# Conv-attention layer and displaced blur: key/value units in two halves of each pair, x statistics moved into the projection, one tile of layer 1 per pair

## The reference

```python
# layer 0: x = x + attention(group_norm(x))
qkv = x_flat @ W_qkv.T            # 12 heads of 64; q is not used
var_v = jnp.var(v, axis=-1, ddof=1, keepdims=True)
var_k = jnp.var(k, axis=-1, ddof=1, keepdims=True)
scores = var_v @ jnp.swapaxes(var_k, -2, -1) * scale      # rank one: 1024 x 1024 per head
out = jax.nn.softmax(scores, axis=-1) @ v
out = out @ W_proj.T + b_proj
# layer 1: x = x + displace(group_norm(x)): each channel is shifted by whole pixels
# (zeros outside), then a 3 x 3 Gaussian with a sub-pixel centre is applied to it
```

## Time and profile before

| what | value |
|---|---|
| median of 3 runs | 2242.65 us (2242.59 to 2244.2) |
| profiled execution, its own time | 2248.03 us |
| its span, first to last instruction | 2246.5 us |
| mean granted TensorE clock | 0.959 |
| PE busy | 2061.6 us, 92% |
| PEld busy | 1101.4 us, 49% |
| DVE busy | 1680.9 us, 75% |
| ACT busy | 1179.2 us, 52% |
| POOL busy | 145.9 us, 6% |
| DMA, mean | 98 GB/s, 219.14 MB |

### The profile page before, as it was taken

The page is one execution under the profiler, slowest core; times in us unless marked ns, Lnnn a source line. Parts: engine busy times, 40 slices in busy tenths (PEclk is TensorE's granted clock), DMA queues, the critical chain, the costliest instruction groups (busy, mean ns, idle before and its releaser), DMA issues.

```text
span 2246.5 us, 36318 instructions
## 1 busy us (share of the span) xinstructions
PE 2061.6 (92%) x13036; PEld 1101.4 (49%) x13036; DVE 1680.9 (75%) x3695; ACT 1179.2 (52%) x1285; POOL 145.9 (6%) x215
## 2 busy tenths in 40 slices
PE   3999999998989999999999999999998999999970
PEld 2655356552655436553465525654365543755330
DVE  7577656886679875898659885788667987598738
ACT  5456625665266662567336662566526665356701
POOL 2000000000000000000001000000000000010001
PEclk7899999999999999999999999999999999999995
DMA  6312302433033511334023340244213341143304
GB/s 236 139 48 58 95 11 95 133 130 99 17 108 122 170 42 39 123 121 154 21 67 123 114 143 11 95 133 142 87 27 106 121 164 39 40 132 123 95 10 168
DMA packets 106990, 219.14 MB, mean 98 GB/s; under 512 B 53025, under 2 KB 53793, under 8 KB 106785
## 3 DMA queue, kind: packets, MB, share of 16 engines
q1 hardware_dynamic: 74816, 100.12, 14.9%
q0 software_dynamic: 25920, 94.38, 12.1%
q10 hardware_dynamic: 6048, 22.02, 2.6%
HBM read 158.28 MB, written 57.80 MB: 96 GB/s over the span
## 4 chain that ended last, share of the span: by engine, by line
PE 76%; DMA 7%; DVE 7%; ACT 3%; issue 3%; SPq 3%; ACTq 0%; DVEq 0%; POOL 0%; POOLq 0%
PE ps L1105 30%; PE ps L1144 25%; PE ps L1159 15%; PE ps L1126 5%; ACT ring L599 2%; DMA dt_sb<-d_sb 2%; DMA a_sb<-a_rows 2%; SPq L461 1%; DMA a_rows<-at 1%; DVE xv L859 1%; DVE xv L861 1%; DVE st L754 1%; SPq L400 1%; DVE bt L805 1%; DMA xv<-in_L_conv_W_qkv 1%
## 5 line engine op out<-in xcount | busy, mean ns | idle before, releaser
L599 ACT ACTIVATE ring<-a_sb,coef 128x1024 f32<-128x1024 f32 x768 | 834.3, 1139 | 404.7 <-PE ps L1144 215.7
L1105 PE MATMUL ps<-wkv_hi,h_sp 128*128 128x256 f16 x4608 | 806.2, 278 | 46.9 <-ACT xv L583 39.5
L1144 PE MATMUL ps<-ring,xv 128*64 128x512 f32 x3072 | 739.6, 612 | 0.7
L1105 PE MATMUL ps<-wkv_lo,h_sp 128*128 128x256 f16 x2304 | 639.7, 278 | 0.0
L1105 PEld LDWEIGHTS ps<-wkv_hi,h_sp 128*128 128x128 f16 x4608 | 458.4, 99 | 214.3 <-issue 122.5
L805 DVE TENSOR_TENSOR bt<-bt,ring 128x1024 f32<-128x1024 f32 x416 | 487.7, 1214 | 1.8 <-issue 1.8
L1144 PEld LDWEIGHTS ps<-ring,xv 128*64 128x64 f32 x3072 | 196.7, 138 | 381.2 <-issue 359.7
L1159 PE MATMUL ps<-xv,wp_hi 128*128 128x512 f16 x1152 | 347.4, 379 | 10.0 <-issue 9.6
L754 DVE BATCH_NORM_STATS2 st<-ps 128x6 f32<-128x64 f32 x1536 | 219.8, 217 | 116.5 <-PE ps L1105 115.6
L583 ACT ACTIVATE xv<-ps 128x256 f32<-128x256 f32 x192 | 70.9, 369 | 351.8 <-DVE st L754 351.6
L1105 PEld LDWEIGHTS ps<-wkv_lo,h_sp 128*128 128x128 f16 x2304 | 229.2, 99 | 28.9
(11 more groups left out here) (122 smaller groups left out, 1329.6 us busy)
## 6 DMA issues: line engine op xcount, KB each, us to landing
a_sb<-a_rows SPq DMA_DIRECT2D x96, 512.0 KB, 5.9
xv<-in_x POOLq DMA_DIRECT2D x48, 512.0 KB, 3.7
bt<-r_rows SPq DMA_DIRECT2D x96, 256.0 KB, 3.9
h_sp<-in_x ACTq DMA_DIRECT2D x42, 512.0 KB, 6.5
shift_rows<-bt POOLq DMA_DIRECT2D x42, 512.0 KB, 2.9
out<-xv POOLq DMA_DIRECT2D x42, 512.0 KB, 3.6
shift_rows<-ring SPq DMA_DIRECT2D x12, 528.0 KB, 14.8
xv<-in_L_conv_W_qkv SPq DMA_DIRECT2D x4, 1152.0 KB, 9.2
```

The source lines that it names most:

```text
L599: nc.scalar.activation(ring_of(p, s, m), a_sb[:, h % 4, :], ACT.Exp, scale=coef[:, h, m:m + 1]).then_inc(s_exp, 1)
L1105: last = nc.tensor.matmul(ps[:, kv_bank[u % 2], half * 2 * P:(half + 1) * 2 * P], h_sp[:, k, hp, m * P:(m + 1) * P], wkv[wpart][:, k, q * ...
L1144: last = nc.tensor.matmul(ps[s * HD:(s + 1) * HD, o_bank[p % 2] + j, :], v_sb[:, p, m, s * HD:(s + 1) * HD], ring_of(p, s, m)[:, j * HALF: ...
```

## The change

In pairs 0 to 3, PE makes two units, multiplies m = 0 to 3, makes two units, multiplies m = 4 to 7 (before: one unit after each of m = 0, 2, 4, 6). The transposes come before m = 0 (before: after m = 1), the spread after m = 2 (before: after m = 3). Unit 6 is evicted in phase A. ACT evicts units in twos at steps 3 and 7, DVE takes their statistics at steps 2, 3, 5 and 6 and makes the variances two pairs ahead at step 6. `k_max` moves from step 2 to step 3, behind an add and a unit's statistics. Tile p of layer 1 is done in pair p, at steps 3 and 6. `add_bias` moves to step 7, for tile 4 to the span's end. The six loads of the next x are issued in twos at steps 1, 4 and 7 of pair 4. The statistics of x move from pair 5 to the start of the projection, around the last reciprocal, and the DMAs of their chain on SP behind the last broadcast of r. `o_second` of a pair comes at step 7 of the next. The projection first takes k = 0 to 3 of units 2 to 5, then k = 4 of all six.

```diff
--- before.py
+++ after.py
@@ -429,14 +429,12 @@
                     r_broadcast(b, p - 1, later)
                     if p < NP - 1:
                         a_broadcast(b, p + 1, later)
+                d_rows(b, NP - 1)
+                r_write(b, NP - 1)
+                r_broadcast(b, NP - 1, later)
                 if with_next:
                     stats_to_groups(sp, "x", b + 1)
-                d_rows(b, NP - 1)
-                r_write(b, NP - 1)
-                if with_next:
                     stats_out(sp, "x", b + 1)
-                r_broadcast(b, NP - 1, later)
-                if with_next:
                     stats_to_channels(sp, "x", b + 1)

             def first():
@@ -571,8 +569,8 @@
                     if t:
                         h_first(b, t - 1)

-            def load_x(b):
-                for t in range(CT):
+            def load_x(b, tiles):
+                for t in tiles:
                     act.dma_start(x_in[:, t, :], x_t[b, :, t, :]).then_inc(s_xin[t], 16)

             def v_evict(b, u):
@@ -623,7 +621,7 @@
                 nc.scalar.activation(t_t, g_t, ACT.Copy, scale=taps[:, t, 1, 1:2]).then_inc(s_tap, 1)

             def phase_a(b, beside=None):
-                for u in range(2 * UQ - 2):
+                for u in range(2 * UQ - 1):
                     v_evict(b, u)
                     if beside is not None:
                         beside(u)
@@ -631,42 +629,39 @@
             def span(b, l1, with_next, beside=None):
                 later = l1 is not None
                 for p in range(NP):
-                    nxt = (p + 1) * UQ
+                    nxt = (p + 2) * UQ
                     for m in range(MT):
                         if not later and p == 0 and m == 3:
                             act.wait_ge(s_pads, 2 * CT * 16)
                         exps(b, p, m)
-                        if m == 0 and 1 <= p <= 4:
-                            v_evict(b, nxt + 1)
-                        if m == 1 and p == 0 and later:
-                            middle_tap(l1, 0)
-                        if m == 2 and p <= 4:
-                            v_evict(b, nxt + 2)
+                        if m == 1 and p == 0:
+                            v_evict(b, 2 * UQ - 1)
                         if m == 3:
                             if p:
                                 d_copy(b, p - 1, later)
-                            if p <= 4:
-                                v_evict(b, nxt + 3)
-                            if p == 4 and with_next:
-                                load_x(b + 1)
-                        if m == 4 and 1 <= p <= 4 and later:
-                            middle_tap(l1, p + 1)
-                        if m == 5 and p:
-                            add_bias(b, p - 1)
-                        if m == 6 and p <= 3:
-                            v_evict(b, nxt + UQ)
+                            if later:
+                                middle_tap(l1, p)
+                            if p <= 3:
+                                v_evict(b, nxt)
+                                v_evict(b, nxt + 1)
                         if m == 7:
                             if p:
                                 o_first(b, p - 1)
-                            elif later:
-                                middle_tap(l1, 1)
+                            if 1 <= p <= 4:
+                                add_bias(b, p - 1)
+                            if p <= 3:
+                                v_evict(b, nxt + 2)
+                                v_evict(b, nxt + 3)
+                        if with_next and (p, m) in ((4, 1), (4, 4), (4, 7)):
+                            load_x(b + 1, (2 * (m // 3), 2 * (m // 3) + 1))
                         if beside is not None:
                             beside(p, m)

             def span_end(b, later):
                 d_copy(b, NP - 1, later)
+                add_bias(b, CT - 2)
+                o_first(b, NP - 1)
                 add_bias(b, CT - 1)
-                o_first(b, NP - 1)

             def weight_first(u):
                 parts, sc, t, k, r, bank = w_unit(u)
@@ -684,7 +679,7 @@
             def beside_span(p, m):

                 if (p, m) == (0, 0):
-                    for w in range(2 * (2 * UQ - 2 - 2), WU - WKU):
+                    for w in range(2 * (2 * UQ - 1 - 2), WU - WKU):
                         weight_first(WKU + w)
                 if (p, m) == (1, 0):
                     act.wait_ge(s_sub, 1)
@@ -887,65 +882,55 @@
             def span(b, l1, with_next, beside=None):
                 later = l1 is not None
                 for p in range(NP):
-                    nxt = (p + 1) * UQ
-                    if p >= 2:
-                        o_second(b, p - 2)
-                    if p <= 4:
-                        kv_stats(b, nxt + 3)
-                        variances(b, p + 1)
+                    nxt = (p + 2) * UQ
+                    if p == 0:
+                        kv_stats(b, 2 * UQ - 1)
+                        variances(b, 1)
                     for m in range(MT):
                         add_up(b, p, m, later)
-                        if m == 1 and p == 5 and with_next:
-                            x_stats(b + 1, (0, 1))
                         if m == 2:
                             if p:
                                 d_reciprocal(b, p - 1)
+                            if p <= 3:
+                                kv_stats(b, nxt)
+                        if m == 3:
+                            if p <= 3:
+                                kv_stats(b, nxt + 1)
                             if p <= 4:
                                 k_max(b, p + 1, later)
-                            if p == 0 and later:
-                                taps_y(l1, 0, g_t, t_t)
-                                gn(l1, 1, g_t)
-                                taps_x(l1, 0, t_t)
-                            if p == 5 and with_next:
-                                x_stats(b + 1, (2, 3))
-                        if m == 3:
-                            if p <= 3:
-                                kv_stats(b, nxt + UQ)
-                            if p == 5 and with_next:
-                                x_stats(b + 1, (4, 5))
-                                channel_aggregate("x", b + 1)
+                            if later:
+                                taps_y(l1, p, g_t, t_t)
+                                if p + 1 < CT:
+                                    gn(l1, p + 1, g_t)
                         if m == 4:
+                            if p <= 4:
+                                k_scales(b, p + 1)
                             if p:
                                 o_normalise(b, p - 1)
-                            if p <= 4:
-                                k_scales(b, p + 1)
-                        if m == 5:
-                            if p <= 3:
-                                kv_stats(b, nxt + UQ + 1)
-                            if 1 <= p <= 4 and later:
-                                taps_y(l1, p + 1, g_t, t_t)
-                                if p + 2 < CT:
-                                    gn(l1, p + 2, g_t)
+                        if m == 5 and p <= 3:
+                            kv_stats(b, nxt + 2)
                         if m == 6:
                             if p <= 3:
-                                kv_stats(b, nxt + UQ + 2)
-                            if p == 0 and later:
-                                taps_y(l1, 1, g_t, t_t)
-                                gn(l1, 2, g_t)
-                            if p <= 4 and later:
-                                taps_x(l1, p + 1, t_t)
+                                kv_stats(b, nxt + 3)
+                                variances(b, p + 2)
+                            if later:
+                                taps_x(l1, p, t_t)
+                        if m == 7 and p:
+                            o_second(b, p - 1)
                         if beside is not None:
                             beside(p, m)

             def group_end(b, with_next):
-                o_second(b, NP - 2)
+                if with_next:
+                    x_stats(b + 1, range(4))
+                d_reciprocal(b, NP - 1)
+                if with_next:
+                    x_stats(b + 1, (4, 5))
+                    channel_aggregate("x", b + 1)
+                o_normalise(b, NP - 1)
+                o_second(b, NP - 1)
                 if with_next:
                     group_var(dve, "x", b + 1)
-                d_reciprocal(b, NP - 1)
-                if with_next:
-                    group_spread_x(dve, b + 1, H_UP)
-                o_normalise(b, NP - 1)
-                o_second(b, NP - 1)
                 for u in range(PU):
                     t, j = divmod(u, 2)
                     dve.wait_ge(s_pj, b * PU + u + 1)
@@ -954,8 +939,10 @@
                     cut = x1[:, t, j * HALF:(j + 1) * HALF]
```

(29 more changed lines are left out.)

## The result

| | before | after |
|---|---|---|
| median | 2242.62 us (4 runs, 2239.26 to 2244.2) | 2203.53 us (4 runs, 2201.6 to 2208.88) |
| profiled execution, its span | 2248.03, 2246.5 us | 2203.28, 2201.7 us |
| mean granted TensorE clock | 0.959 | 0.965 |
| PE, DVE, ACT busy | 92%, 75%, 52% | 92%, 76%, 53% |

The ratio of the new time to the old is 0.9831 [0.9811, 0.9852]: faster, as predicted, and inside the range. The sum was made for the profiled execution, 2203.5 us, and that took 2203.28; the forecast for the median, 2198, is 5 us low. In the second set of runs, on the chip of the first experiments, the same kernel gave 0.9854. The experiments are set against the ratio of the same set of runs where there is one, else against 0.984, the middle of the two; 0.001 is 2.2 us. The two ratios of the changed kernel lie 0.0023 apart, so a difference against 0.984 is known to some 3 to 5 us only.

The account below looks back on a forecast made before the run. PE, 92% busy, waited for V and `kdiag`; after the change the DVE-ACT-rows loop sets pairs 1 to 4. Six middle batches -39.3, last +1.7, batch 0 -6.9: -44.5, so 2203.5 us profiled, 2198 median; range 2170 to 2236.

Parts of the forecast that it names:

- The loop: Pairs 1 to 4: DVE from the reciprocal, ACT exponentials, `d_copy`, row DMAs, next reciprocal; 33.6 us against PE's 32.5; chance 0.58.
- After `kdiag`: Pair 4: from `kdiag` to the pair's end 15.8 us, before 14.1, with one product more behind it.
- The merging pays nothing there: Pairs 1 to 4: PE's merged runs make a pair 32.5 instead of 33.4 us, but the loop sets the pace.
- The early eviction: Pair 0: `v_evict` 6 moved ahead of the exponentials, so unit 8 needs nothing more; pair 0 takes 32.5 instead of 40.4.
- The load term: Pair 4: two loads of the next x meet the denominators' rows and lengthen their trip by 1.2 us, bounds 0 and 3.8.
- Projection and phase A: Start of a batch: 73.6 us plus 0.5, as the late subtraction readies tile 5 1.9 after the projection's end.
- The last batch: Batch 7, which has no load: 258.4 us, before 256.7, so +1.7.
- Batch 0: No layer 1, PE sets its pairs: -7.9 in pair 0, -0.9 x 3, +3.7 in pair 4, together -6.9 us.
- The x statistics: Twelve statistics, 7.9 us with aggregation, move from pair 5 to the projection, mostly hidden; +0.5 us with the start between.
- Full merging: Rival: the merging pays in full if `kdiag` is no later than before, 254.9 us a batch, 2157 in all; chance 0.08.
- Late r rows: Rival: r rows late behind the moved `a_write`, `o_normalise` stops DVE; 2261 with DVE held 3 us each pair; chance 0.09.
- A late x chain: Rival: x's chain has some 6 us before `h_second` waits, 7 us per us beyond; slower from 12 late, 2250; chance 0.03.

## Why the prediction was right, point by point

| stretch of batch 3 | before | predicted | after |
|---|---|---|---|
| projection and phase A | 73.6 | 74.1 | 76.8 (795.06 to 871.85) |
| pairs 0 to 4 | 166.1 | 160.2 | 158.0 (to 1029.83) |
| pair 5 | 25.3 | 25.3 | 26.1 (to 1055.94) |
| mean of six middle batches | 266.2 | 259.6 | 260.1 |
| batch 0, against before | | -6.9 | -7.5 |
| last batch | 256.7 | 258.4 | 255.9 |

The stretch of batch 3 starts with the projection of batch 2. In sum -44.5 predicted and -44.8 by the spans. It is partly luck. In batch 3 the forecast for pairs 0 to 4 is 2.2 us too long, that for projection and phase A 2.7 and that for pair 5 0.8 too short. The six middle batches together were forecast 3 us too short, the last one 2.5 too long and batch 0 0.6 too long.

- **The loop** was right, term by term: forecast 28.1 from reciprocal to `d_copy` and 5.5 for the trip, measured 27.9 and 5.7, 5.2; in sum forecast 33.6, measured 33.5 and 33.0, and 34.8 with the loads as forecast. Lengthening it costs time, a step less of exponentials in it gains. So was pair 0 (32.5 forecast and measured) and the size of the wait (7 to 8 named as the longest, though the working gives 144.4 - 135.5 = 8.9; 7.50 here and 8.57 at most in pair 4, 55.5 in all where some 60 was said). Pair 1's reciprocal was forecast 39.4 after pair 0's start and came at 38.6, the spread was forecast at 144.4 and ran at 143.1 (1014.94 - 871.85).
- **After `kdiag`** 15.8 us were forecast to the end of pair 4; it is 1029.83 - 1014.94 = 14.9. That and the 1.3 us before are the 2.2 us of pairs 0 to 4.
- **"The merging pays nothing there"** was wrong. It was costed by PE's own time only, 0.9 us a pair, which the loop hides. But the order of the units also sets when the loop starts. Undone, the start is 3.8 us later, the three rounds after it are 2.0 longer, and the whole is 43 us longer. The sum held because it was made with the new order's start.
- **The early eviction** was a side remark of the prediction, inside the 7.9 us of pair 0. It carries the change: 57 us by taking it out, and all the gain by putting it alone into the kernel before. The prediction put pair 0's waits down to DVE's two tiles; that holds for the second wait only, the first was for unit 6 behind the exponentials. The 57 and the 43 of the merging add up to far more than the change's 39. They can't be added: with either one taken out the changed kernel is slower than the kernel before (1.0094 and 1.0047), so its other parts cost time in that state; which of them do was not taken apart.
- **The load term** was forecast at 1.2 over a trip of 5.5; the trip is 7.0, 1.5 over. Without loads beside it, it is 4.7. This agrees with what the Trainium skill ("DMA: Bandwidth & Descriptors", Issuing engines are not separate DMA queues) says of DMAs issued by different engines, that they run on the same 16 DMA engines.
- **Projection and phase A** is the term that was mis-sized: +0.5 forecast, +3.2 measured in batch 3. Some 2.1 lie in the projection: either its 192 products take 43.28 instead of 41.61, or, as in this batch, the last `o_second` is late (1.88). The prediction saw the last `o_second` ready 0.4 us ahead of PE's need (1095.1 against 1095.5), took both from the trace of before, and gave the term nothing. In the changed kernel PE waited for it in four batches, 6.2 us in all; that is one of the prediction's own signs of being wrong. `o_normalise` of pair 5 waits for the r rows, and `o_second` follows it. The rest lies ahead of phase A's first units, with waits of 0.3 to 0.7 for `h_sp` and for V.
- **Pair 5** is 0.8 longer, and the idle time ahead of the projection, which is counted in it, is 2.54 instead of 1.64.
- **The last batch** was forecast 1.7 longer, and is 0.8 shorter. Its four row trips took 4.2, 5.8, 4.8 and 4.8 us where the loop had 5.5 each: 2.5 less, as much as the forecast was off.
- **Batch 0** has the right size with a wrong reason in pair 0: -7.9 was taken over from the other batches, and its pair 0 ended 8.1 earlier (126.84 instead of 134.98). But no tile of layer 1 stands there; before, PE had waited 2.41 us for a part of the weights and 2.41 for V.
- **The x statistics** were costed at 0.5 a batch; moving them back costs 8 us in all, so the move gains.
- **The rivals.** Full merging (2157) would have needed `kdiag` on time. Late r rows: in pairs 1 to 4 of batches 1 to 7 `o_normalise` did not wait for them; the 46.2 us lie in batch 0, in pair 5 and behind it. A late x chain: 11.2 us of waits for `h_second` in 13, where the kernel with the early eviction alone has 9.6 in 6; in the middle batches 0.34 each, under the 1 us that was named as a sign of being wrong.

## What to carry to other kernels

Where work goes round a loop over several queues (here DVE, ACT, SP and DVE again), cost the loop and its starting point, not the engine that is 92% busy: a new order on PE can pay by making the loop start sooner, and here a step taken out of the loop paid 24 us, one reordered at its end 17. Before a large reordering, try each of its small moves alone in the old kernel; here one did it all. A wait removed at the end of a late chain comes back at the next reader of the same chain: ask who else reads it.

## What the runs showed of the hardware

Whether a short idle time of PE is followed by a stretch at half the clock depends on more than its length. Ahead of a key/value unit in pair 0, an idle time of 2.2 us was followed by a unit of 5.76 us in the kernel before and of 4.09 us in the kernel with the eviction alone (893.13), while there the same idle time of 2.22 in another batch was followed by 5.71 (1416.96). By stretches (window: us, PE busy with instructions, granted clock as a share of 2.4 GHz, DMA share, GB/s), the kernel before and then both places of the one with the eviction alone:

```profile
913.10:916.40 3.30, 3.29 (x21) 0.65 0.83 217
```

```profile
893.10:896.00 2.90, 2.87 (x27) 1.00 0.84 191
...
1416.96:1419.90 2.94, 2.94 (x14) 0.50 0.73 155
```

In the changed kernel the 192 products after an idle time of 2.54 took 43.28 us, with the first 3 us at the lower level, 1.2 GHz:

```profile
1055.90:1058.90 3.00, 2.96 (x8) 0.50 0.21 32
```

Such a stretch costs 1.6 to 1.7 us and stands in no list of waits. In the kernel with `d_copy` early the idle time was 1.65 and the products took 41.62:

```profile
1045.57 41.62 PE ps L1146 x192
```
